# AdaLN, recurrent mixing and routed feed-forward on one Trainium2 core: the expert table's up-projection rows laid out by quarters and fetched in two halves, and a new order of work on every engine

## The reference

```python
mod = (silu(c) @ wmod).reshape(32, 6, 1, 256)          # sa ca ga sb cb gb
h = layernorm(x) * (1 + ca) + sa
s_t = a * s_(t-1) + (1 - a) * h_t                       # a = sigmoid(decay_logit), per channel
x = x + ga * (S @ W + b + depthwise_conv5(h) + conv_b)
h = layernorm(x) * (1 + cb) + sb
e = argmax(softmax(gelu(h[last token] @ Wp1 + bp1) @ Wp2 + bp2))     # one expert of 8 per row
y = gelu(h @ W1[e] + b1[e]) @ W2[e] + b2[e]
x = x + gb * (h + 0.3 * (y @ Wo + bo))
```

## Time and profile before

| | |
|---|---|
| median of 3 runs | 654.22 us (653.48 to 655.22) |
| the profiled execution's own time | 653.61 us |
| its span, first to last instruction | 651.8 us |
| PE busy | 633.2 us (97%) |
| DVE busy | 568.0 us (87%) |
| ACT busy | 551.1 us (85%) |
| POOL busy | 439.4 us (67%) |
| granted TensorE clock | 0.998 of full speed |

### The profile page before, as it was taken

The page is one execution under the profiler, slowest core; times in us unless marked ns, Lnnn a source line. Parts: engine busy times, 40 slices in busy tenths (PEclk is TensorE's granted clock), DMA queues, the critical chain, the costliest instruction groups (busy, mean ns, idle before and its releaser), DMA issues.

```text
span 651.8 us, 11098 instructions
## 1 busy us (share of the span) xinstructions
PE 633.2 (97%) x3405; PEld 521.6 (80%) x3405; DVE 568.0 (87%) x895; ACT 551.1 (85%) x976; POOL 439.4 (67%) x536
## 2 busy tenths in 40 slices
PE   7898899999999999999999999999999999999996
PEld 7686687888788888888888888888888888888865
DVE  1686889999899999999999999999999999998712
ACT  3797788889888988889988988888988898887763
POOL 2774676776677676776667667677666767677543
PEclk9999999999999999999999999999999999999999
DMA  9999635455445455455544545554544455543442
GB/s 297 329 358 298 212 135 194 139 186 167 166 158 191 162 193 194 148 185 175 172 165 163 189 167 194 176 185 158 194 146 170 171 175 183 193 162 111 172 165 104
DMA packets 55454, 120.58 MB, mean 185 GB/s; under 512 B 5643, under 2 KB 43364, under 8 KB 46180
## 3 DMA queue, kind: packets, MB, share of 16 engines
q1 hardware_dynamic: 51844, 115.65, 51.9%
q10 hardware_dynamic: 3552, 4.23, 2.0%
HBM read 61.12 MB, written 25.19 MB: 132 GB/s over the span
## 4 chain that ended last, share of the span: by engine, by line
PE 84%; DMA 7%; POOL 3%; DVE 2%; ACT 2%; issue 1%; SPq 1%; DVEq 0%; ACTq 0%; POOLq 0%
PE U L1062 10%; PE U L1063 9%; PE U L1064 9%; PE Q L1077 9%; PE Q L1078 8%; PE Q L1082 8%; PE TR L1102 8%; PE Q L1094 4%; PE Y L1046 4%; PE Y L1043 4%; PE Y L1042 4%; PE TR L1094 4%; DMA up_w<-up_table 3%; DMA xr<-in_L_attn_x_dram 2%; DMA xr<-in_L_ffn_W_dram 2%; PE U L1117 2%
## 5 line engine op out<-in xcount | busy, mean ns | idle before, releaser
L452 POOL TENSOR_TENSOR g_lo<-g,g_hi 128x512 fp32r<-128x512 f32 x128 | 173.8, 1358 | 90.0 <-ACT g_hi L613 85.0
L839 DVE SCALAR_TENSOR_TENSOR Y<-h,taps,Y 128x512 f32<-128x512 f32 x320 | 224.7, 750 | 2.9 <-PE Y L1046 0.7
L1062 PE MATMUL U<-hid_hi,up_w 128*128 128x512 f32 x256 | 107.4, 419 | 2.2 <-DMA up_w<-up_table 2.2
L1077 PE MATMUL Q<-g_hi,down_w 128*128 128x512 f32 x256 | 106.2, 415 | 0.0
L565 ACT ACTIVATE S<-xr,nmr,rstd 128x256 f32<-128x256 f32 x128 | 66.6, 592 | 42.6 <-POOL S_lo L460 40.1
L1063 PE MATMUL U<-hid_hi,up_w 128*128 128x512 f32 x256 | 101.4, 396 | 0.0
L1078 PE MATMUL Q<-g_hi,down_w 128*128 128x512 f32 x256 | 101.1, 395 | 0.0
L1064 PE MATMUL U<-hid_lo,up_w 128*128 128x512 f32 x256 | 100.8, 394 | 0.0
L787 DVE BATCH_NORM_STATS2 st<-xr 128x6 f32<-128x512 f32 x128 | 88.4, 712 | 9.4 <-DMA xr<-in_L_attn_x_dram 4.9
L606 ACT ACTIVATE g<-U,up_w 128x512 f32<-128x512 f32 x128 | 88.1, 688 | 8.6 <-PE U L1064 7.0
L435 POOL TENSOR_SCALAR rstd<-st 128x4 f32<-128x4 f32 x64 | 26.5, 413 | 87.2 <-DVE st L787 84.5
(11 more groups left out here) (115 smaller groups left out, 1293.7 us busy)
## 6 DMA issues: line engine op xcount, KB each, us to landing
up_w<-up_table SPq DMA_DIRECT2D x32, 1027.0 KB, 6.2
down_w<-down_tab SPq DMA_DIRECT2D x32, 1024.0 KB, 4.7
xr<-in_L_attn_x_dram SPq DMA_DIRECT2D x32, 512.0 KB, 3.6
out_dram<-xr SPq DMA_DIRECT2D x64, 256.0 KB, 2.3
xr<-in_L_ffn_W_dram ACTq DMA_DIRECT2D x5, 512.0 KB, 11.6
xr<-in_L_ffn_W_dram SPq DMA_DIRECT2D x4, 512.0 KB, 9.4
up_table<-g_lo SPq DMA_DIRECT2D x2, 1024.0 KB, 10.2
up_table<-down_w SPq DMA_DIRECT2D x2, 1024.0 KB, 9.3
```

Source lines behind the costliest of these rows:

```text
L452: nc.gpsimd.tensor_tensor(g_lo[:, f], g[:, f % 2], g_hi[:, f].bitcast(f32), ALU.subtract).then_inc(g_lo_ready, 1)
L839: ins = nc.vector.scalar_tensor_tensor(out=Y[c][:, :], in0=h[:, c, k:k + T], scalar=taps[:, c, k:k + 1], in1=Y[c][:, :], op0=ALU.mult, op1 ...
L1062: mm(U[f % 2][:, :], up_w[:, par, UP + w:UP + w + P], hid_hi[:, par, c], start=(c == 0), stop=False)
L1077: mm(Q[c][:, :], down_w[:, par, 1, w:w + P], g_hi[:, f], start=(f == 0), stop=False)
```

## The change

1. **Table.** In a row of `up_table` b1 and beta now come first (6 numbers), then W1 by quarters of the hidden width: for each quarter f the high part (2 x 128), then the low part (2 x 128). `w1_hi` and `w1_lo` write, and `up` reads, in that layout.
2. **Fetch.** `fetch` is cut in two. `fetch_up` reads the row in two DMAs: b1, beta and quarters 0 and 1 (semaphore `up_half_loaded`), then quarters 2 and 3 (`up_loaded`). `up(i,0)` and `gate_beta` wait for the first, `up(i,2)` for the second. `fetch_up(i+1)` stands ahead of the load of row i+5, `fetch_down` behind it.
3. **Order in the slots**, and 4. **order in the prologue**, as in the diff.

```diff
-    U_B1 = 2 * UP
+    U_B1 = 0
     U_BETA = U_B1 + FC
-    UPW = U_BETA + DC
+    U_W = U_BETA + DC
+    UPW = U_W + 2 * UP
+    U_HALF = U_W + UP
...
+        def by_f(room):
+            return room.rearrange("p (f k c n) -> p f k c n", k=2, c=DC, n=P)
...
             def prologue():                                  (SP)
+                load_x(0)
                 vectors()
+                load_w1(0)
                 load_w2(0)
+                load_wo()
                 load_w()
-                load_x(0)
-                load_wo()
+                load_w2(1)
+                load_w1(1)
                 load_taps()
-                load_router()
-                load_w1(0)
-                load_w1(1)
-                load_w2(1)
                 load_x(1)
                 sp.wait_ge(s_mod_mm, 1)
                 load_w2(2)
-                b1_out()
                 load_w1(2)
+                load_w1(3)
                 sp.wait_ge(s_mod_mm, 1)
                 load_x(2)
                 split_out(0)
-                load_w1(3)
                 sp.wait_ge(s_wT, 1)
                 load_w1(4)
+                beta_out()
+                b1_out()
                 split_out(1)
+                split_out(2)
                 load_w1(5)
                 load_w1(6)
-                split_out(2)
                 split_out(3)
-                split_out(4)
-                beta_out()
+                load_router()
                 sp.wait_ge(s_w2T_mm, 4)
                 load_w1(7)
+                split_out(4)
                 split_out(5)
-                split_out(6)
                 sp.wait_ge(s_w1_lo, E)
                 load_x(3)
+                split_out(6)
                 split_out(7)
...
-                sp.dma_start(up_w[:, par].bitcast(f32), up_table[bass.ds(e, 1)]...).then_inc(up_loaded[par], 16)
+                table = up_table[bass.ds(e, 1)].rearrange("o p n -> p (o n)")
+                sp.dma_start(up_w[:, par, 0:U_HALF].bitcast(f32), table[:, 0:U_HALF]).then_inc(up_half_loaded[par], 16)
+                sp.dma_start(up_w[:, par, U_HALF:UPW].bitcast(f32), table[:, U_HALF:UPW]).then_inc(up_loaded[par], 16)
...
+                if row(i + 1):
+                    e = fetch_up(i + 1)
                 if row(i + 5):
                     load_x(i + 5)                            (after its wait for the store)
                 if row(i + 1):
-                    fetch(i + 1)
+                    fetch_down(i + 1, e)
...
             def slot(i):                                     (POOL)
                     norm2(i + 1)
-                    norm1(i + 4)
-                    gate_beta(i)
                     g_low(i, 0)
                     g_low(i, 1)
                     hid_low(i + 1)
+                    norm1(i + 4)
                     g_low(i, 2)
                     g_low(i, 3)
+                    gate_beta(i)
                     s_low0(i + 3)
...
             def slot(i):                                     (ACT)
                     gelu(i, 1)
+                    g_high(i, 1)
                     hid_of(i + 1)
-                    g_high(i, 1)
                     hid_high(i + 1)
+                    nav_of(i + 1)
                     gelu(i, 2)
-                    nav_of(i + 1)
                     h_of(i + 3)
                     gate1(i + 2)
                     g_high(i, 2)
-                    gelu(i, 3)
                     s_high(i + 3, 0)
+                    gelu(i, 3)
                     g_high(i, 3)
-                    gate2(i)
                     s_high(i + 3, 1)
+                    gate2(i)
...
             def slot(i):                                     (DVE)
                     output(i - 1)
-                    conv(i + 2, 0, 2)
+                    conv(i + 2, 0, 4)
                     stats1(i + 4)
-                    conv(i + 2, 2, 7)
+                    conv(i + 2, 4, 8)
                     residual2(i - 1)
-                    conv(i + 2, 7, TAPS * DC)
+                    conv(i + 2, 8, TAPS * DC)
+                    scan(i + 3, 0)
                     router(i + 1)
-                    scan(i + 3, 0)
                     scan(i + 3, 1)
                     residual1(i + 2, 0)
...
             def slot(i):                                     (PE)
                     router_logits(i + 1)
                     up(i, 3)
-                    down(i, 1)
                     back_to_tokens(i + 2)
+                    down(i, 1)
                     down(i, 2)
                     down(i, 3)
```

More of the change, by code:

```diff
@@ L505, in prologue @@
                 norm1(1)
-                s_low0(0)
                 w1_lo(1)
                 w1_lo(2)
+                s_low0(0)
+                w1_lo(3)
                 gates()
-                w1_lo(3)
                 norm1(2)
+                s_low0(1)
                 w1_lo(4)
-                s_low0(1)
                 norm2(0)
@@ L923, in prologue @@
                 down_low(5, 0)
+                stats1(3)
                 down_low(5, 1)
                 scan(2, 0)
+                down_low(6, 0)
                 scan(2, 1)
-                stats1(3)
-                down_low(6, 0)
+                router(0)
                 down_low(6, 1)
-                router(0)
+                down_low(7, 0)
                 residual1(1, 0)
+                s_low1(2)
                 residual1(1, 1)
-                s_low1(2)
-                down_low(7, 0)
                 down_low(7, 1)
```

145 lines of the change are left out of this document (74 added, 71 removed).

## The result

Measured in one comparison, the changed kernel takes 663.91 us (median of 4 runs, 659.67 to 666.20) and the kernel before 653.85 (4 runs, 652.08 to 655.22). The ratio is 1.0145, with a 95% interval of 1.0121 to 1.0169. So it is slower, as forecast, but by 10 us and not by 3.8, and the top of the range (664) was just about the middle of the runs. The profiled execution is the shortest of the four: 659.67 us, span 657.9.

What follows compares the result with a forecast made beforehand. PE's own instructions were taken to set the slots. 653.61 (profiled execution) + 8.3 (slots) - 3.0 (prologue) + 0.3 (row 4) - 1.8 (end) = 657.4; the median lies 0.6 higher: 658.0 us, range 647 to 664.

Steps and rivals of the forecast that it cites:

- The loop that sets the slots: Slots: mix, taps, gate1, transposes, down 1-3, next mix form a closed loop; PE stalls 0.30 to 0.70 us each.
- the floor: Slots: the least stall of PE ahead of the transposes, 0.30 us per slot, +5.1 us in total.
- 0.42: Slots: stall taken per slot, blocking between DVE and POOL included; 27 times it, less 3.0 of small waits, gives +8.3.
- All these at nothing: Slots: the other moves (router, `gate_beta`, `fetch_up`, extra DMA) cost nothing, bounds 0 to 0.1 us per slot.
- The prologue: Sum of the prologue's parts, with (a), (b) and (c) in it: -3.0 us, from -5.0 to +2.0.
- (b): Prologue: the last W1 load leaves some 4 us earlier, the table (complete at 68.5) and fetch sooner: -2.0 us.
- (a): Prologue: the first up product waits for half a row, 3.3 us at best, instead of 4.87: -1.6 us.
- Rival E: Prologue: halves do nothing, PE not ready earlier or DMAs share engines with row 4; 661.5 us, chance within main case's 0.58.
- rival D: Slots: DVE and POOL block each other, 0.70 us each, no prologue gain: 668.3; sign: first up product past 75; chance 0.08.
- (c): Prologue: 3.6 of PE's 5.0 us idle between 40 and 80 must go; 0.6 of that counted as not gone.
- Slot 0: Row 4, loaded behind the fetch, may hold `stats1(4)`: +0.3 us, 0 to +1.
- The end: Last slots: earlier transposes and second norm, fewer waits, half row for the last up product: -1.8 us, from -2.7 to 0.

Runs made afterwards that it cites:

- e2: The kernel before with only PE's new slot list (transposes back to tokens ahead of down 1): 659.18 us, slots of 18.43.
- e14: The kernel before with only DVE's new slot list (router behind the first scan, taps divided 4, 4, 2): 663.05 us.
- e13: The kernel before with only ACT's new slot list: 658.56 us, slots of 18.33.
- e15: The kernel before with only POOL's new slot list (`norm1` behind `hid_low`, `gate_beta` behind `g_low(i,3)`): 725.99 us.
- e1: The changed kernel with PE's old slot list (transposes back to tokens behind down 1 again): 667.58 us, slots of 18.49.
- e6: The changed kernel with all slot lists of before; table, halves, fetch and prologue stay new: 658.07 us.
- e7: e6 with one DVE item, `down_low(2, 1)`, moved ahead of `scan(1, 0)` and `stats1(2)` in the prologue: 656.98 us.
- e8: e1 with `gate_beta` ahead of `g_low(i,0)` again on POOL: 662.53 us, slots of 18.33.
- e10: e8 with `hid_of` ahead of `g_high(i,1)` again on ACT: 671.4 and 673.7 us in two of six runs, the others 694 to 695.
- e3: The kernel before with only the new table layout and the fetch in halves, all orders of before: 657.03 us.
- e12: The kernel before with PE's move in the slots from 28 on only: 653.87 us, ratio 0.9974 to 1.0006.
- e4: The changed kernel with the prologues of all engines in the order of before; layout, halves and slots stay new: 661.79 us.

## Why the prediction was right and wrong

**The loop that sets the slots: right.** The wait is where it was put, behind `gate1` and ahead of the transposes into TR, and the length from first tap to `gate1` was exact. e2 shows it alone: 5.9 us for the 27 slots.

**Its size: the floor, not 0.42.** In the slot above PE stalls 0.25 us; the floor was 0.30, which gives 18.10 + 0.30 = 18.40 for a slot, and I took 0.42, with 0.12 on top for blocking between DVE and POOL. The term was +8.3 and measured +6.4. By the floor it would have been +5.1; the other 1.3 us are in the main what six slots (1, 14, 17, 18, 20 and 25, with 18.47 to 18.92) take above 18.40, so not all of the 3.0 of small waits went. The blocking is there (the scan of 1.73 us), but DVE then still waits 0.84 for PE at `output`: it is covered, as the prediction said a delay under 0.4 would be, and the cover was larger than that.

**"All these at nothing": wrong, though it did not show in the sum.** DVE's list costs 9 us alone (e14), ACT's 4.5 (e13), POOL's 72 (e15). In the changed kernel they cost nothing on top of PE's move (18.45 against 18.43 in e2), because slots are set by the longest loop and not by a sum. But the argument for each zero looked only at the reader of the moved result. It did not ask what the scans would lie beside: the prediction had them 0.40 us earlier, and the first one is 1.29 earlier, at 10.96 us after the mix in place of 12.25. Nor did it ask what stands queued behind `gate2` on ACT, or which engine waits for the statistics behind four taps. It also means that "undo PE's move" would not have won the slots back (e1), which I expected.

**The prologue: the step that failed.** Forecast -3.0. It is +1.0 in the changed kernel's trace, and +3.4 by the medians (e6). Of this the layout is about 1, the halves about 1, the new orders about 1, each a difference of medians that is hardly clear of the noise.

(b) held the fetch to the completion of the table. It waits for the choice of the expert: the choice's last instruction and the fetch behind it, in the kernel before and in the changed one, from the timelines of DVE and SP:

```profile
69.16 0.15 DVE L882 FIND_INDEX8 sel<-top,logits 1x8 uint32<-1x8 f32 x1
```

```profile
68.74 0.15 DVE L900 FIND_INDEX8 sel<-top,logits 1x8 uint32<-1x8 f32 x1
```

```profile
69.96 0.36 SPq L403 DMA_DIRECT2D up_w<-up_table  x1
```

From the end of the first to the fetch it is 70.39 - 69.31 = 1.08 us, from the end of the second 69.96 - 68.89 = 1.07, and in each of the 16 traces 1.07 or 1.08. The table was complete 1.9 us before the fetch (68.5, the prediction's own sum), in the changed kernel 2.3 (58.65 + 9.0 = 67.7). The last W1 load did leave 5.2 us earlier (39.31, before 44.52), and the fetch only 0.43. That load is tied to the choice by another way, through the load of row 3, which SP issues when the last `w1_lo` is done; DVE's `stats1(3)`, and behind it the low half that PE's next product waits for, need that row. In the kernel before, from the chain and from DVE's timeline:

```profile
60.25 4.26 DMA xr<-in_L_attn_x_dram
```

```profile
62.08 2.33 DVE L888 TENSOR_TENSOR_SCAN S<-keep,h 128x512 f32<-128x512 f32 x2
```

The row landed at 64.51 and DVE was in its scans until 64.41. So by this way an earlier load alone could win 0.1 us there.

(a) counted 1.6 us for the half row, from the shortest load of 512 KB. The first half landed in 3.9 us, 1.0 sooner than the whole row's 4.87. And PE is only ready for the first up product when its mix is done; in the changed kernel that product stands at 74.20, not "near 72", and 1.10 ahead of 75.30. Rival E had named this, and its 661.5 is the nearest of the forecasts. In the other traces with the new prologue and the halves (e1, e6, e7, e8, e10) the product stands at 76.2 to 79.1, later than before; that was the prediction's sign for rival D, whose slots did not come. Even the 1.10 is lost again in slot 0, where PE waits for `hid_of` of row 1, a wait that the kernel before does not have:

```profile
81.38 0.61 PE L1139 MATMUL U<-w_raw,wp 128*128 128x1 f32 x4 [1.58 <-ACT w_raw L668]
```

(c) had 3.0 of the idle time gone. It moved: 1.9 more ahead of 60 us, 2.9 less behind, with part of the busy time at a lower clock. That the prologue's lists, dense on all engines, would bring a new long wait was in no step.

**Slot 0 and the end.** Slot 0 was put at +0.3: -0.1 in the changed kernel, +0.9 in e3, where `stats1(4)` waits for row 4, as named beside that term. The end was put at -1.8 and gave -1.2; e2 and e12 have the same 68.8 us, so it is PE's move alone.

**The sum.** -1.9 on the slots, +0.6 at the end and +6.1 in the prologue with slot 0 (from -2.7 to e6's +3.4) make 4.8 of the difference of 5.9 between 658.0 and 663.9. The last 1.1 I can't place: the four runs of the changed kernel spread over 6.5 us (those of before over 3), and only the shortest has a trace. It may lie in the prologue, whose new orders cost 3.0 us beside the new slots (e4) and 1.0 beside the old (e6 less e3), but the noise doesn't allow to say so.

## What to carry to other kernels

When several engines' lists are closed into one loop, the slot is the longest of several loops: a step that is free in a sum can be the next limit, and undoing the guilty step may win nothing. Check for each moved instruction not only who reads its result but what it now runs beside on an engine that shares its port, and what is queued behind anything that it waits for. For a gated start, look for the last of all its conditions in the trace (here the choice, 1.07 or 1.08 us ahead in every trace) before pricing an earlier one.

## What the runs showed that I had not expected

- DVE's new list alone (the router's small instructions, 0.6 us together, behind the first scan, and two more taps ahead of the statistics) cost 9 us, since both scans then met long instructions of POOL's: 1,711 ns in the mean instead of 1,324.
- `hid_of` ahead of one cast of 0.6 us on ACT made a slot 0.4 us longer (e8 to e10), and the kernel's runs fell into two groups, 671 to 674 and 694 to 695 us. No trace shows the second group.
- Stores of the table that begin 24 bytes into a row of DRAM landed in 11.0 to 13.6 us, those that begin at column 0 in 7.7 to 10.1 (medians of two stores, in nine and in seven traces; six of the nine also have the new prologue).
- A pause of PE of 2.85 us in the prologue was followed by a granted clock of 0.59 between 40 and 44 us, and a group of matmuls took 3.34 us in place of 1.97. A pause of 2.20 us elsewhere was not followed by a lower clock.
